# Row maxima copied by ScalarE and split by GpSimd, and the last residual summed by TensorE

## The reference

```
xn   = layernorm(x)
sim  = q @ k.T + bias(i - j) * SCALE          # per head, causal
y    = x + softmax(sim) @ v @ Wo.T + bo
t    = layernorm(y)
z    = t + relu(t @ w1 + b1) @ w2 + b2
out  = y + (z - mean(z)) * rsqrt(var(z) + 1e-5) * gamma + beta
```

## Time and profile before

| | us |
|---|---|
| median of 3 runs | 321.29 |
| lowest, highest | 316.94, 323.11 |
| the profiled execution | 316.09 |
| its span | 314.0 |

### The profile page before, as it was taken

How to read it: one execution, slowest core, us unless ns; L and a number is a source line. 1 busy time by engine, 2 the same in 40 slices (tenths; PEclk the granted TensorE clock), 3 DMA queues, 4 the chain that set the end, 5 groups by cost and what they waited for, 6 DMA issues and landing times. The chain is left out here.

```text
span 314.0 us, 8361 instructions
## 1 busy us (share of the span) xinstructions
PE 277.9 (88%) x3242; PEld 116.3 (37%) x3244; DVE 273.7 (87%) x970; ACT 191.4 (61%) x265; POOL 89.8 (29%) x141
## 2 busy tenths in 40 slices
PE   8977697799989998998999899899979989999990
PEld 3443322223332342243334233333422333368760
DVE  4886769989999999999999999999999966838896
ACT  2275406777567668666767866675675678742450
POOL 7169699912202020220211022022000010704420
PEclk9999959969999999999999999999999999999997
DMA  8536756102201120120102233222112011000022
GB/s 212 167 104 155 181 169 177 52 3 62 59 4 41 24 62 2 60 62 3 54 13 64 30 82 73 33 69 56 46 26 38 3 27 28 2 6 13 0 68 67
DMA packets 16311, 18.80 MB, mean 60 GB/s; under 512 B 4656, under 2 KB 11952, under 8 KB 16144
## 3 DMA queue, kind: packets, MB, share of 16 engines
q1 hardware_dynamic: 13376, 14.00, 18.1%
q0 software_dynamic: 2560, 3.68, 4.2%
q10 hardware_dynamic: 336, 0.61, 0.8%
HBM read 11.81 MB, written 4.23 MB: 51 GB/s over the span
## 5 line engine op out<-in xcount | busy, mean ns | idle before, releaser
L752 ACT ACTIVATE PT<-ps 128x1024 f32<-128x1024 f32 (+1 forms) x192 | 144.9, 811 | 73.2 <-PE ps L1243 66.9
L908 DVE TENSOR_REDUCE FM<-ps 128x1 f32<-128x512 f32 (+2 forms) x192 | 109.0, 617 | 4.9 <-PE ps L1205 2.7
L915 DVE CUSTOM_DVE_ANT_0 junk<-ps,NBH 128x256 bf16<-128x256 f32 (+1 forms) x256 | 88.8, 402 | 10.7 <-PE ps L1205 9.5
L1205 PE MATMUL ps<-KA,QA 56*128 56x256 bf16 (+3 forms) x544 | 72.5, 289 | 16.7 <-DVE FM L908 8.5
L1255 PE MATMUL ps<-PT,VG 128*16 128x512 f32 (+3 forms) x768 | 82.7, 495 | 0.1
L1225 PE MATMUL ps<-QA,KA 58*128 58x512 bf16 (+3 forms) x384 | 57.1, 334 | 3.6 <-ACT PT L752 2.6
L396 POOL DMA_DIRECT2D KA<-qk_scratch x32 | 17.2, 543 | 139.0 <-PE ps L1243 131.8
L1205 PEld LDWEIGHTS ps<-KA,QA 56*128 56x128 bf16 x544 | 24.4, 95 | 82.4 <-DVE FM L908 35.2
L1243 PE MATMUL ps<-TT,flb 128*32 128x176 f16 (+4 forms) x1152 | 40.2, 243 | 0.0
L1225 PEld LDWEIGHTS ps<-QA,KA 58*128 58x128 bf16 x384 | 18.4, 95 | 34.2 <-ACT PT L752 24.6
L1243 PEld LDWEIGHTS ps<-TT,flb 128*32 128x32 bf16 x1152 | 20.5, 95 | 19.9 <-issue 19.4
(11 more groups left out here) (107 smaller groups left out, 251.2 us busy)
## 6 DMA issues: line engine op xcount, KB each, us to landing
QA<-qk_scratch SPq DMA_DIRECT2D x64, 48.0 KB
KA<-qk_scratch POOLq DMA_DIRECT2D x32, 96.0 KB, 2.7
qk_scratch<-QS SPq DMA_DIRECT2D x9, 128.0 KB
qk_scratch<-QS SPq DMA_DIRECT2D x6, 192.0 KB, 3.6
X<-in_x SPq DMA_DIRECT2D x4, 256.0 KB, 5.6
PT<-fr_scratch SPq DMA_DIRECT2D x1, 1024.0 KB, 4.6
OT<-f_scratch SPq DMA_DIRECT2D x2, 480.0 KB, 6.7
xnT<-OT SPq DMA_DIRECT2D x28, 32.0 KB
```

Source lines behind the costliest of these rows:

```text
L752: nc.scalar.activation(PT[:, s % 3, 2 * q:2 * q + 2, off:off + w], ST[:, q, :, off:off + w], ACT.Exp).then_inc(s_exp, 1)
L908: nc.vector.tensor_reduce(FM[:, ib, heads[0]:heads[-1] + 1:2, piece], bank[:, 0:w * len(heads)].rearrange("p (h n) -> p h n", n=w), AX.X, ...
L915: last = nc.vector.tensor_tensor_reduce(junk[:, n % NSM, i, 0:w], bank[:, i * w:(i + 1) * w], nb[:, h, 256 - w:256], 1.0, NEG, ALU.add, AL ...
L1205: last = nc.tensor.matmul(SM[:, POS[g, k] % NSM, at:at + nj], QA[r0:r0 + KS, p, ib // 4, q, (ib % 4) * 128:(ib % 4 + 1) * 128], KA[r0:r0 + ...
```

## The change

For groups 1 to 7, the rounding of the maxima and the difference move from VectorE to GpSimd (`split_maxima`), and the copy of the transposed row moves from VectorE to ScalarE (`copy_row`), which places it ahead of the exponentials of the next step or behind them, by the place of the unit in the table. Banks that ScalarE frees are counted by two new semaphores (`s_mrow`), and whoever needs a bank asks `left_bank`. The table is changed between units 0 and 20 and for units 34, 38 and 39; the table of group 0 stays.

In the last stage, for quarters 2 and 3 (`ON_PE = 2`), ScalarE writes the transposed tile with b2 added back into T2, and TensorE adds its transpose to the output bank with one more matmul for each tile of 128 columns, against the identity. The additions of b2 and the sums into Z go for these quarters; statistics and the first scaling read the bank.

```
 UNITS_AT = {
-    (0, 1): [(0, (40,)), (1, (0, 1))], (1, 0): [(0, (41,)), (1, (2, 3))], (1, 4): [(1, (4,))], (2, 0): [(1, (5,))],
-    (2, 1): [(1, (6,))], (2, 4): [(1, (7, 8))], (3, 2): [(1, (9, 10)), (1, (11, 12))], (4, 3): [(1, (13, 14))],
-    (5, 1): [(1, (15,)), (1, (16,))], (5, 4): [(1, (17,)), (1, (18,))], (6, 0): [(1, (19, 20))],
...
-    (8, 4): [(1, (29, 30))], (9, 0): [(1, (31, 32))], (9, 4): [(1, (33,))], (10, 1): [(1, (34, 35))],
-    (11, 0): [(1, (36, 37))], (11, 3): [(1, (38, 39))],
+    (0, 1): [(0, (40,)), (1, (0,)), (1, (1,))], (1, 0): [(0, (41,)), (1, (2, 3))], (1, 4): [(1, (4,))],
+    (2, 0): [(1, (5,))], (2, 1): [(1, (6,))], (2, 4): [(1, (7, 8))], (3, 4): [(1, (9, 10))], (4, 0): [(1, (11,))],
+    (4, 4): [(1, (12, 13))], (5, 0): [(1, (14, 15)), (1, (16,))], (5, 4): [(1, (17,)), (1, (18, 19))],
+    (6, 0): [(1, (20,))], (6, 4): [(1, (21, 22))], (7, 0): [(1, (23, 24))], (7, 4): [(1, (25, 26))],
+    (8, 0): [(1, (27, 28))], (8, 4): [(1, (29, 30))], (9, 0): [(1, (31, 32))], (9, 4): [(1, (33,))],
+    (10, 0): [(1, (34, 35))], (11, 0): [(1, (36, 37))], (11, 3): [(1, (38,))], (11, 6): [(1, (39,))],
 }
+def by_scalar(g, k):
+    return g > 0 and UNITS[k][0] == "m"
+def reduced(n):
+    return sum(not by_scalar(*gk) for gk in STREAM[:max(n + 1, 0)])
+ON_PE = 2
...
+        def left_bank(eng, n):
+            if n >= 0 and by_scalar(*STREAM[n]):
+                g, k = STREAM[n]
+                eng.wait_ge(s_mrow[UNITS[k][1]], g)
+            else:
+                eng.wait_ge(s_smf, NSM + reduced(n))
...
@@ GpSimd
+            def split_maxima(g, half):
+                v = 2 * (g - 1) + half
+                nm3 = NM[:, half, :].rearrange("p (i q e) -> p i e q", q=HP, e=2)
+                m0, m1 = (MC[:, half, :, :, q, :] for q in range(2))
+                pool.wait_ge(s_nm, v + 1)
+                nc.gpsimd.tensor_copy(m0, nm3).then_inc(s_mc, 1)
+                pool.wait_ge(s_mc, v + 1)
+                nc.gpsimd.tensor_tensor(m1, nm3, m0, ALU.subtract).then_inc(s_ms, 1)
             for g in range(G - 1):
                 p = g % 2
                 if g:
                     pool.wait_ge(s_str, 2 * NSTEP * g)
                     load_k(pool, g + 1, 1 - p, 1, s_ldk)
+                    split_maxima(g, 1)
+                split_maxima(g + 1, 0)
...
@@ ScalarE
+            def copy_row(g, half):
+                act.wait_ge(s_smr, POS[g, row_of(half)] + 1)
+                bank = SM[:, POS[g, row_of(half)] % NSM, :]
+                nc.scalar.copy(mrow[:, half, :], bank.bitcast(BF16)[0:8, 0:IC]).then_inc(s_mrow[half], 1)
...
                 for s in range(NSTEP):
+                    rows_of_maxima(g, s, False, last)
...
                     if s + 1 < NSTEP:
                         exps(g, s + 1)
                     elif not last:
                         exps(g + 1, 0)
+                    rows_of_maxima(g, s, True, last)
...
                     nc.scalar.copy(tT[:, c % 2, :], bank).then_inc(e_tTs, 1)
+                    if c >= ON_PE:
+                        nc.scalar.activation(T2[c], bank, ACT.Identity, bias=cols[:, 2:3]).then_inc(e_tc, 1)
...
@@ VectorE
+                if by_scalar(g, k):
+                    return
...
+                    if g:
+                        nc.vector.tensor_reduce(nm, fm, AX.X, ALU.max, negate=True).then_inc(s_nm, 1)
+                        return
...
-                dve.wait_ge(e_pe["t"], 4)
-                t = T2[3].rearrange("p (t d) -> p t d", d=D)
-                nc.vector.tensor_tensor(t, t, rows[:, 4:5, :].broadcast_to([128, 4, D]), ALU.add).then_inc(e_tb, 1)
...
+                if c >= ON_PE:
+                    stats(lambda i: bank[:, i * 128:(i + 1) * 128], c, e_v3, tiles)
+                    return
...
@@ TensorE
-                pe.wait_ge(s_smf, n + 1)
+                left_bank(pe, n - NSM)
...
                     for k, (i, f) in enumerate((i, f) for i in tiles for f in range(4)):
+                        if f == 0 and c >= ON_PE:
+                            pe.wait_ge(e_tc, c + 1 - ON_PE)
+                            nc.tensor.matmul(bank[:, i * 128:(i + 1) * 128], T2[c][:, i * 128:(i + 1) * 128], idf[:, :],
+                                             start=True, stop=False, skip_group_check=True)
```

More of the change, by code:

```diff
@@ L167, with maxima_at @@
 }
+def by_scalar(g, k):
+    return g > 0 and UNITS[k][0] == "m"
+def reduced(n):
+    return sum(not by_scalar(*gk) for gk in STREAM[:max(n + 1, 0)])
+def maxima_at(table):
+    out = {}
+    for (s, gap), jobs in table.items():
+        for own, ks in jobs:
+            if UNITS[ks[0]][0] == "m":
+                out.setdefault((s, gap >= 2), []).append((own, UNITS[ks[0]][1]))
+    return out
+ON_PE = 2
 WITHIN = [("y", 0), ("t", 0), ("h0", 0), ("y", 1), ("h1", 0), ("t", 1), ("h2", 0), ("h3", 0),
@@ L344, in build @@
         s_ms = sem("s_ms")
+        s_nm = sem("s_nm")
+        s_mc = sem("s_mc")
+        s_mrow = [sem(f"s_mrow{i}") for i in range(2)]
         s_md = [sem(f"s_md{i}") for i in range(2)]
@@ L362, in build @@
         e_hs = sem("e_hs")
+        e_tc = sem("e_tc")
         e_tb = sem("e_tb"); e_xb = sem("e_xb")
@@ L454, in move_m @@
             def move_m(p, half, g):
-                sp.wait_ge(s_smf, POS[g, NU - 1 if half else M0] + NSM + 1)
+                left_bank(sp, POS[g, row_of(half)])
                 for e in range(2 if g else 1):
@@ L758, in sums, with rows_of_maxima @@
                                OV[:, :]).then_inc(s_ov, 1)
+            def copy_row(g, half):
+                act.wait_ge(s_smr, POS[g, row_of(half)] + 1)
+                bank = SM[:, POS[g, row_of(half)] % NSM, :]
+                nc.scalar.copy(mrow[:, half, :], bank.bitcast(BF16)[0:8, 0:IC]).then_inc(s_mrow[half], 1)
+            def rows_of_maxima(g, s, behind, last):
+                for own, half in maxima_at(UNITS_AT if g else UNITS_AT0).get((s, behind), []):
+                    if g + own and not (own and last):
+                        copy_row(g + own, half)
             def group(g, last=False, first=False):
                 for s in range(NSTEP):
+                    rows_of_maxima(g, s, False, last)
                     if first and s == FIRST_STEP[1] - 1:
-                        act.wait_ge(s_smf, POS[0, NU - 1] + NSM + 1)
+                        left_bank(act, POS[0, NU - 1])
                         move_row(act, 1, 0, 1, s_mda[1])
@@ L1028, in scaled @@
                 for i in tiles_of(c, half):
-                    z, u = (a[:, c % 2, i * 128:(i + 1) * 128] for a in (Z, U))
+                    u = U[:, c % 2, i * 128:(i + 1) * 128]
+                    z = (Z[:, c % 2, :] if c < ON_PE else ffn_bank(c, half))[:, i * 128:(i + 1) * 128]
                     last = nc.vector.scalar_tensor_tensor(u, z, mv[:, 4 * c + i, 0:1], rows[:, 2, :],
@@ L1194, in job @@
                     return
-                pe.wait_ge(s_smf, POS[g, ks[-1]] + 1)
+                for k in ks:
+                    left_bank(pe, POS[g, k] - NSM)
                 pieces = [pieces_of(k) for k in ks]
@@ L1265, in task @@
                     pe.wait_ge(s_late, 16)
-                    pe.wait_ge(s_smf, NSM + NU * G)
+                    for i in range(NSM):
+                        left_bank(pe, len(STREAM) - 1 - i)
                 if BANKS2[n] >= 6 and n < len(WITHIN) + 8:
@@ L1274, in task @@
                     else:
-                        pe.wait_ge({"y": e_x1, "t": e_tTs, "o": e_z, "p": e_z}[k], cm + 1)
+                        by = {"y": e_x1, "t": e_tTs, "o": e_z, "p": e_z}[k]
+                        late = cm >= ON_PE and k in "top"
+                        assert not (late and k in "op")
+                        pe.wait_ge(e_tc if late else by, cm + 1 - ON_PE * late)
                 if kind == "y":
@@ L1294, in task @@
                         last = nc.tensor.matmul(bank[:, i * 128:(i + 1) * 128], hidden(c, f)[:, i * 128:(i + 1) * 128],
-                                                w2_s[:, f, :], start=(f == 0), stop=(f == 3), skip_group_check=True)
+                                                w2_s[:, f, :], start=(f == 0 and c < ON_PE), stop=(f == 3),
+                                                skip_group_check=True)
                 last.then_inc(e_pe[kind[0]], 1)
```

20 lines of the change are left out of this document (13 added, 7 removed), and 1 row of the table UNITS_AT.

## The result

| | before | after |
|---|---|---|
| median, us | 319.37 (4 runs, 316.94 to 323.11) | 311.82 (4 runs, 311.43 to 313.64) |
| profiled execution, us | 316.09 | 311.59 |
| its span, us | 314.0 | 309.7 |

What follows compares the result with a forecast made beforehand. VectorE and the loop over ScalarE were taken to bind the groups almost equally, VectorE's chain the tail. Attention 2.6 plus tail 2.0 gave 4.6 us, ratio 0.9854: 316.6 us from 321.29, range 310.5 to 323.0.

Steps and rivals of the forecast that it cites:

- Two things of nearly the same length: Attention groups: VectorE's work and the loop of exponentials, scores and biases both bind; 0.3 us gained in each of groups 1 to 5.
- A: Whole kernel, the forecast: two bounds of one length, 316.6 us; groups 1 to 5 at 26.6 to 27.1; chance 0.60.
- B: Rival for the attention: VectorE is the only bound, groups 1 to 5 at 25.6 us, total 309.7 us; chance 0.18.
- The step on ScalarE: Between steps 5 and 6: a row copy of 0.59 us delays step 6; the 1.14 us gap before step 7 absorbs 0.4.
- the new positions of the units: I take zero: Attention: units 9 to 20 move by up to one step, TensorE does the same matmuls, so no effect.
- Bound by VectorE: 1.2 of 1.5: Group 6: VectorE is the bound outright there, so 1.2 us of the 1.5 taken from it is gained.
- the 0.50 us that the scores of step 4 wait: Group 7: read as waiting for the row's transfer; a later row was taken to cost 0.3 us, at most 0.5.
- The 0.6 us from maxima to MC: GpSimd's cast and difference with semaphore crossings: 0.6 us against 0.35 before, covered by VectorE's remaining reductions.
- whether GpSimd slows VectorE: Attention: whether GpSimd's new instructions lengthen VectorE's beside them; the cost was taken as zero.
- The 2.23 us derived from the order: Last stage on VectorE: 1.33 us from earlier statistics and 0.45 from each half of the last quarter.
- The loss of 0.2 for reading the bank: Last stage: statistics and scaling read the bank instead of SBUF; 0.2 us lost, bound 1.0.
- The margin of TensorE's last bank: Tail: TensorE's added matmuls end at 306.86, 0.5 us before VectorE needs the last bank at 307.35.

Runs made afterwards that it cites:

- the second copy: The changed kernel with ScalarE copying the row of the first half's maxima twice in groups 0 to 6; group 5 took 27.41 us against 26.95.

## Why the prediction was right, and where it was not

*What bounds a group.* "Two things of nearly the same length, and a gain on one alone is worth little": on VectorE's side this is shown. 0.3 us was taken for each of groups 1 to 5, 0.10 to 0.19 came, 0.7 in all for 1.5. A further relief of VectorE by 8 us a group gives only 0.2 more. That the loop over ScalarE is the other bound is argued from its gaps (0.71 to 0.73 us before step 7) and from the second copy; no run made the loop shorter. VectorE's busy time fell to 24.84 us, between the 24.4 given for A and the 25.6 given for B; by the lengths, 26.95, it is A.

*The step on ScalarE.* The copy took 0.57 us for the 0.59 taken, the gap before step 7 went to 0.73, as said. Its net was read too simply, as time moved from one engine to another. The step of the reasoning that failed is "the new positions of the units: I take zero". With the changed engines the new places are worth 0.68 us a group (27.63 to 26.95), with the old ones they cost 0.47; the difference of these, 1.15 us, is what places and engines do only together.

*Group 6.* "Bound by VectorE: 1.2 of 1.5": 0.16 came. That was the mis-sized term of the sum. VectorE's busy time in it fell by 0.94 us and its idle time rose by 0.8 (from 0.6 to 1.4). Group 6 is longer by the reciprocals, as read, but by what stands behind each of them in the order of the banks, not by VectorE's total.

*Group 7.* 0.13 us lost for 0.3, and not by the way that was read. The prediction took the 0.50 us that the scores of step 4 wait as a wait for the row's transfer, which a later row would lengthen. These scores start 6.11 us into the group, before 5.97, and wait the same 0.50:

```profile
254.51 0.31 PEld L1299 LDWEIGHTS ps<-QA,KA 58*128 58x128 bf16 x4 [0.50 <-DMA QA<-mrow]
```

With the reciprocals moved, the transfers are issued 2.84 us into the group (249.94), 0.36 later than before the change (2.48, 252.80), and yet the scores start at 5.96 after the same 0.50 us, now put down to nothing that the profile shows:

```profile
253.06 0.31 PEld L1302 LDWEIGHTS ps<-QA,KA 58*128 58x128 bf16 x4 [0.50 <-issue]
```

So before the change they did not wait for the row. What is longer after the change stands ahead of them, on GpSimd, TensorE and ScalarE:

```profile
249.51 0.59 POOL L667 CAST MC<-NM 128x16 bf16<-128x16 f32 x1 [19.41 <-DVE NM L993]
250.55 0.38 PE L1248 MATMUL ps<-idb,MC 128*8 128x128 bf16 x4 [0.27 <-POOL MC L669]
250.97 0.57 ACT L813 COPY mrow<-ps 8x512 bf16<-8x512 bf16 x1 [0.20 <-PE ps L1248]
```

GpSimd's rounding takes 0.59 us here, beside a product of VectorE with two inputs (249.37 to 250.05), where its median is 0.20. The transposes wait for it, the copy waits for the transposes, and the next exponentials start 3.22 us into the group in place of 3.08. With the reciprocals moved VectorE runs those in this place, and the rounding takes 0.20:

```profile
248.22 0.20 POOL L668 CAST MC<-NM 128x16 bf16<-128x16 f32 x1 [18.32 <-DVE NM L994]
```

The copy then waits for nothing, the next exponentials start at 3.07, and group 7 takes 29.49 us, where it took 29.50 before the change.

*GpSimd.* Two instructions of 0.20 and 0.22 us (medians) in the place of 0.28 each. The 0.6 us from maxima to MC was right within 0.1 (201.79 to 202.35); before it was 0.43 (203.38 to 203.81), not the 0.35 of the prediction. The transposes were covered in group 5, but not in group 7 (above). The prediction asked whether GpSimd slows VectorE, and took zero; what it did not ask is whether VectorE slows GpSimd.

*The tail.* The 2.23 us derived from the order are there. The loss of 0.2 for reading the bank is not, and 0.3 us come on top. The wait for GpSimd is 0.31 for 0.45 us. And a product of VectorE runs alone now. Beside it GpSimd had been adding a row to X1 for quarter 2; without the addition of b2 ahead of it, that work is done earlier. In the kernel with the attention's changes alone, VectorE and GpSimd:

```profile
287.26 0.82 DVE L1034 TENSOR_TENSOR XN<-XN,xnT 128x512 f32<-128x512 f32 x1
...
286.26 1.28 POOL L705 TENSOR_TENSOR QS<-QS,rows 128x512 f32<-128x512 f32 x1
```

and the same product after the whole change:

```profile
286.35 0.69 DVE L1038 TENSOR_TENSOR XN<-XN,xnT 128x512 f32<-128x512 f32 x1
```

The margin of TensorE's last bank is 0.26 us for the 0.5 forecast, since VectorE wants the bank sooner by these 0.3.

What reading the bank costs is in the statistics and the first scaling, by source (ns min/median/max, first and last start):

```profile
L1103 DVE SCALAR_TENSOR_TENSOR U<-Z,mv,rows x8: 319/346/348, 290.8 to 297.3; 128x128 f32<-128x128 f32 x8
L1103 DVE SCALAR_TENSOR_TENSOR U<-ps,mv,rows x8: 341/342/352, 300.7 to 306.4; 128x128 f32<-128x128 f32 x8
...
L1043 DVE BATCH_NORM_STATS2 st<-Z x8: 275/276/295, 287.7 to 294.9; 128x6 f32<-128x128 f32 x8
L1043 DVE BATCH_NORM_STATS2 st<-ps x8: 279/282/295, 299.4 to 305.5; 128x6 f32<-128x128 f32 x8
```

4 ns less for the scaling and 6 more for the statistics. The estimate of 65 ns for every such instruction, worked out from the Trainium skill, "VectorE: DVE Perf Modes", section on the TRN2 errata, is not in these rows; the measurement decides, and the rule would have taken 0.8 us of the forecast wrongly away.

*The total.* Too much by 1.7 in the attention and too little by 0.5 in the tail leaves 3.4 us for 4.6 in the stages that the change touches, a ratio of 0.989; the measured ratios are 0.9857 and 0.9845, and the intervals hold 0.989. That the measured ratio met the forecast 0.9854 so closely is luck: errors of opposite sign met, and what the stages show is 0.989.

## What to carry to other kernels

Where three buffers go round between two in-order engines, ask of every operation moved to another engine not what it costs there, but when its buffer comes free and who stands behind it; the place in the issue order and the engine are one decision, and each half of it alone can lose. An extra operation on an engine is nearly free in a spot where that engine waits anyway, and costs much of its length elsewhere: 2.2 us of reciprocals in group 6 cost 0.1 us (and the 1.8 us moved to group 7 nothing), where all 3.8 us in group 6 had cost 2.0. A busy share of 95% did not make VectorE the bound, and taking away 8 us of its work showed that faster than any reading. And what the profile names as the end of a wait is to be tested: the 0.50 us put down to a transfer stayed the same when the transfer had 0.36 us less time.

## What the hardware showed unexpectedly

The same start takes very different times in single executions. The stretch up to the copy of the first half's sums of group 0, in which the kernels do the same work in the same order: the kernel before, after the change, with the last stage alone, and with before's engines in the new places. The granted clock stands behind GpSimd's busy time:

```profile
0.00:65.64 65.64, 53.20 (x340) 23.05 (x344) 51.02 (x192) 31.31 (x44) 47.99 (x72) 0.89 0.53 146
```

```profile
0.00:64.77 64.77, 52.37 (x340) 23.16 (x344) 51.10 (x192) 31.32 (x44) 47.98 (x72) 0.89 0.53 148
```

```profile
0.00:63.53 63.53, 51.77 (x342) 22.52 (x344) 50.32 (x192) 31.30 (x43) 48.00 (x72) 0.92 0.55 150
```

```profile
0.00:71.28 71.28, 57.83 (x340) 23.93 (x344) 51.92 (x192) 31.37 (x44) 48.03 (x72) 0.80 0.48 134
```

Clock and length go together over 7.8 us, more than twice what the change is worth, while groups 2 to 5 repeat to 0.01 us from run to run where these groups are the same. In the kernel before, the clock is 0.60 from 40 to 50 us, so mostly at the lower of the two levels (1.2 GHz), after 20 us in which TensorE was busy for 7.5 and 7.3 of each 10. So in the profiled executions most of the scatter is made in the first fifth of the kernel; a later stage was hit twice, group 6 of two kernels at 0.94 (29.62 and 30.85 us). An effect of less than a microsecond is to be read from stages of the traces, not from medians.
